# A fused attention and mixture-of-experts stage: the factors' hand-out as two fp32r products, the second layer ahead of the third, single buffers where there were pairs

## What is computed

```
edge_attn = leaky_relu(attn_src[:, src] + attn_dst[:, dst], 0.2)
p         = exp(edge_attn - max)                       # per edge and head
out       = segment_sum(p * h[src], dst) / segment_sum(p, dst)   ; x = x + out + ...
h1 = relu(bn(x @ W1[e])) ; h2 = relu(bn(h1 @ W2[e])) ; y = h2 @ Wo[e] + bo[e]
x  = x + sum_e softmax(mean @ Wr)[e] * y_e             # e = 0..7
```

## Time and profile before

| | |
|---|---|
| median of 3 runs | 6956.88 us (6955.64 to 6963.28) |
| profiled execution, its own time | 6955.62 us |
| its span | 6953.9 us |
| fused stage, about | from 520 to 3920 us of the span |

### The profile page before, as it was taken

The page is one execution under the profiler, slowest core; times in us unless marked ns, Lnnn a source line. Parts: engine busy times, 40 slices in busy tenths (PEclk is TensorE's granted clock), DMA queues, the critical chain, the costliest instruction groups (busy, mean ns, idle before and its releaser), DMA issues. The chain is left out here.

```text
span 6953.9 us, 120698 instructions
## 1 busy us (share of the span) xinstructions
PE 5410.4 (78%) x32110; PEld 4819.8 (69%) x32111; DVE 4435.2 (64%) x11425; ACT 1822.9 (26%) x4253; POOL 4050.3 (58%) x4038
## 2 busy tenths in 40 slices
PE   3427999999999999999999666767676676665887
PEld 2326888888888888888888555555555555554887
DVE  4436888788878787877888444444444454444666
ACT  1301333333333333333333300000000000002554
POOL 0147666666666666666666177777777777773111
PEclk9757999999999999999999877777777777777999
DMA  4545555555455555555555144444444444443221
GB/s 122 159 127 145 139 139 134 141 132 140 131 141 135 137 137 138 136 139 138 134 140 139 38 125 128 126 128 126 128 123 123 122 118 116 118 119 108 75 76 46
DMA packets 655172, 863.42 MB, mean 124 GB/s; under 512 B 283845, under 2 KB 463511, under 8 KB 654122
## 3 DMA queue, kind: packets, MB, share of 16 engines
q0 software_dynamic: 183296, 501.40, 26.8%
q1 hardware_dynamic: 402060, 294.79, 15.3%
q10 hardware_dynamic: 69406, 61.97, 2.7%
HBM read 714.85 MB, written 155.09 MB: 125 GB/s over the span
## 5 line engine op out<-in xcount | busy, mean ns | idle before, releaser
L1228 POOL DMA_INDIRECT m_ring<-tab_a,m_src x1764 | 1965.9, 1114 | 1219.6 <-DMA m_dstb<-dst_p 692.8
L1819 POOL DMA_INDIRECT eb_rows<-tab_b,eb_src x1568 | 1491.8, 951 | 483.6 <-issue 475.9
L1990 PE MATMUL eb_acc<-eb_rows,eb_S 128*128 128x257 f32 x3528 | 1314.0, 534 | 492.8 <-DMA eb_rows<-tab_b,eb_src 477.6
L1990 PEld LDWEIGHTS eb_acc<-eb_rows,eb_S 128*128 128x128 f32 x3528 | 935.2, 280 | 727.5 <-issue 545.3
L1508 PE MATMUL m_acc<-m_V,m_S 128*128 128x264 f32 x3528 | 867.9, 392 | 0.0
L1508 PEld LDWEIGHTS m_acc<-m_V,m_S 128*128 128x128 f32 x3528 | 653.3, 193 | 93.9
L1622 ACT ACTIVATE mh_full<-m_ps,bn_b,bn_s 128x256 f32<-128x256 f32 x784 | 400.0, 561 | 1189.5 <-DVE mh_low L509 942.5
L509 DVE TENSOR_TENSOR mh_low<-mh_full,mh_high 128x512 fp32r<-128x512 f32 x784 | 541.2, 690 | 154.1 <-ACT mh_full L1633 140.6
L1633 ACT ACTIVATE mh_high<-m_ps,bn_b,bn_s 128x256 fp32r<-128x256 f32 x784 | 441.3, 563 | 702.5 <-PE m_ps L521 702.5
L1304 DVE TENSOR_TENSOR m_V<-m_ring,m_V 128x1280 f32<-128x1280 f32 (+1 forms) x392 | 532.5, 1359 | 57.9 <-DVE m_V L1301 0.5
L521 PE MATMUL m_psY<-mWo_low,mh_high 128*128 128x256 f32 x1568 | 350.5, 305 | 255.7 <-issue 240.5
(11 more groups left out here) (348 smaller groups left out, 10716.5 us busy)
## 6 DMA issues: line engine op xcount, KB each, us to landing
m_dstb<-dst_p SPq DMA_DIRECT2D x196, 320.0 KB
m_dstb<-dst_p SPq DMA_DIRECT2D x196, 256.0 KB
buf<-fill SPq DMA_DIRECT2D x49, 771.0 KB
m_ring<-tab_a,m_src POOLq DMA_INDIRECT x1764
eb_rows<-tab_b,eb_src POOLq DMA_INDIRECT x1568, 2.8
xw_stage<-in_L_ffn_w_dram ACTq DMA_DIRECT2D x16, 1024.0 KB, 8.6
over<-b_blank SPq DMA_DIRECT2D x9, 1452.0 KB, 15.1
mOV<-over SPq DMA_DIRECT2D x49, 264.0 KB, 4.4
```

Source lines behind the costliest of these rows:

```text
L1228: gp.indirect_dma_start(out=ring[:, j, :], out_offset=None, in_=scratch["tab_a"], in_offset=bass.IndirectOffsetOnAxis(ap=src[:, j:j + 1], ...
L1819: gp.indirect_dma_start(out=rows_[par][:, to, 0:D], out_offset=None, in_=scratch["tab_b"], in_offset=bass.IndirectOffsetOnAxis(ap=index[:, ...
L1990: return nc.tensor.matmul(ps_acc[par][:, 0:NR], S[par][:, j, :], rows_[par][:, j, :], start=start, stop=False)
```

## The change

1. The factors are split into `q_parts` (high and low, fp32r) in `bounds`: a ScalarE copy and a VectorE subtraction. `ST` becomes fp32r, and `hand_out` does two fp32r products for each edge tile (low, then high) in place of one fp32 matmul.
2. TensorE's order in a step becomes `layer1(e+1)`, `hand_out(e+1)`, [`turn`, `router`], `layer2(e)`, `layer3(e-1)`, `sum_up(e-1)`. In step 0 `layer3` of the previous group goes behind `sum_up`. VectorE's and ScalarE's orders stay.
3. `U` has one buffer (its writer waits for `x1_ok` one group later), `XL` lies in `OV`'s memory (the next `OV` is loaded at step 6 once `turn` has read `XL`, not at step 4), and `fill` is gone: the rows that clear `buf` come from a table in DRAM, `empty`, which `bounds` writes with three more DMAs.

```diff
@@ bounds @@
+            with nc.allow_non_contiguous_dma(reason="one value a row"):
+                for lo, hi, of in ((0, D, blank[:, 0:D]), (D, 2 * D + 1, blank[:, 0:D + 1]), (2 * D + 1, XW, far[:, :])):
+                    sp.dma_start(scratch["empty"][:, lo:hi], of).then_inc(blanked, 16)
...
+            v.wait_ge(q_high, 1)
+            step(k["q_parts"].lower(nc, k["q"][:, 0:NT, :]))
...
+            s.wait_ge(q_ok, 2)
+            nc.scalar.copy(k["q_parts"].high[:, :, :], k["q"][:, 0:NT, :]).then_inc(q_high, 1)
@@ attend_mix, SyncE @@
-                at_least(sp, over_ok, q.n)
+                at_least(sp, T_ok, q.n)
...
-                    if e == 4 and after and not (isinstance(q.n, int) and q.n + 2 >= Q):
+                    if e == 6 and after and not (isinstance(q.n, int) and q.n + 2 >= Q):
                         load(q.next().next())
                     if e == 6:
...
-                                     fill[:, :].rearrange("p (x f) -> p x f", x=1).to_broadcast([P, FILL, XW])).then_inc(filled, 16)
+                                     scratch["empty"].rearrange("p (x f) -> p x f", x=1).to_broadcast([P, FILL, XW])).then_inc(filled, 16)
@@ attend_mix, TensorE @@
                 for j in range(s.size):
-                    last_i = nc.tensor.matmul(psE[s.side][:, j * 16:j * 16 + 2 * H], ST[s.side][:, j, :],
-                                              k["q"][:, bass.ds(s.n, 1), :].rearrange("p x c -> p (x c)"), start=True, stop=True)
+                    for i, part in enumerate(reversed(k["q_parts"].at(bass.ds(s.n, 1)))):
+                        last_i = nc.tensor.matmul(psE[s.side][:, j * 16:j * 16 + 2 * H], ST[s.side][:, j, :],
+                                                  part.rearrange("p x c -> p (x c)"), start=i == 0, stop=i == 1)
...
                     hand_out(Slot(q, e + 1))
-                    if e:
-                        layer3(q, e - 1)
-                    elif before:
-                        layer3(q.prev(), NX - 1)
...
                     if e == 0:
                         sum_up(Slot(q, -1))
+                        if before:
+                            layer3(q.prev(), NX - 1)
                         output_bias(q)
                         layer1(q, 1)
                     layer2(q, e)
                     if e:
+                        layer3(q, e - 1)
                         sum_up(Slot(q, e - 1))
@@ attend_mix, ScalarE @@
-                at_least(s, x1_ok, q.n - 1)
+                at_least(s, x1_ok, q.n)
                 hold(s, passed)
-                nc.scalar.copy(U[q.par][:, j, :], ps_acc[at.par][:, 0:NA]).then_inc(U_ok, 1)
+                nc.scalar.copy(U[:, j, :], ps_acc[at.par][:, 0:NA]).then_inc(U_ok, 1)
```

More of the change, by code:

```diff
@@ L124, in build @@
             k["bn_b"] = [sbuf(first, f"bn_b{i}", [P, NX * KB]) for i in range(2)]
-            k["q"] = sbuf(first, "q", [P, NT + 1, 2 * H])
+            k["q_parts"] = Split(sbuf, first, "q", [P, NT, 2 * H])
             k["corr"] = sbuf(first, "corr", [P, NT, H])
             with ExitStack() as early:
+                k["q"] = sbuf(early, "q_full", [P, NT + 1, 2 * H])
                 k["sd"] = sbuf(early, "sd", [P, NT, 2 * H])
@@ L556, in bounds @@
     blank = sbuf(ctx, "b_blank", [P, NA])
+    far = sbuf(ctx, "b_far", [P, 1])
     node_i = sbuf(ctx, "b_node_i", [P, NT], I32)
@@ L596, in bounds @@
         "cand_ok", "col_ps", "col_ok", "pos_ps", "hot_ok", "list_ps", "list_ok"))
+    q_high = s_("q_high")
     staged, ST_ok, z_ps, z_dv, z_done, dv, passed = map(s_, ("staged", "ST_ok", "z_ps", "z_dv", "z_done", "dv", "passed"))
@@ L660, in _ @@
             rest()
-            sp.wait_ge(blank_ok, 1)
+            sp.wait_ge(blank_ok, 2)
+            with nc.allow_non_contiguous_dma(reason="one value a row"):
+                for lo, hi, of in ((0, D, blank[:, 0:D]), (D, 2 * D + 1, blank[:, 0:D + 1]), (2 * D + 1, XW, far[:, :])):
+                    sp.dma_start(scratch["empty"][:, lo:hi], of).then_inc(blanked, 16)
             for g in range(9):
@@ L664, in _ @@
                              blank[:, :].rearrange("p (x f) -> p x f", x=1).to_broadcast([P, 11, NA])).then_inc(blanked, 16)
-            sp.wait_ge(blanked, 16 * 9)
+            sp.wait_ge(blanked, 16 * 12)
             sp.wait_ge(pp_out, 16)
@@ L730, in _ @@
             nc.vector.memset(blank[:, :], 0.0).then_inc(blank_ok, 1)
+            nc.vector.memset(far[:, :], float(FAR)).then_inc(blank_ok, 1)
             step(nc.vector.memset(zrun[:, :, :], -HUGE))
@@ L1080, in attend_mix @@
     mhalf = sbuf(ctx, "mhalf4", [P, GM])
-    fill = sbuf(ctx, "fill", [P, XW])
     ring = sbuf(ctx, "m_ring", [P, WT, TA])
@@ L1086, in attend_mix @@
     dstb = [sbuf(ctx, f"m_dstb{i}", [P, QUARTERS[i] * P], I32) for i in pair]
-    ST = [sbuf(ctx, f"m_ST{i}", [P, QUARTERS[i], P]) for i in pair]
+    ST = [sbuf(ctx, f"m_ST{i}", [P, QUARTERS[i], P], F32R) for i in pair]
     V = [sbuf(ctx, f"m_V{i}", [P, QUARTERS[i], NA]) for i in pair]
@@ L1092, in attend_mix @@
     node_col = [sbuf(ctx, f"m_col{i}", [P, 1]) for i in pair]
-    U = [sbuf(ctx, f"mU{i}", [P, GM, NA]) for i in pair]
-    OV = sbuf(ctx, "mOV", [P, GM, NA])
+    U = sbuf(ctx, "mU", [P, GM, NA])
     R = [sbuf(ctx, f"mR{i}", [P, GM, D]) for i in pair]
     den = [sbuf(ctx, f"mden{i}", [P, GM, H]) for i in pair]
-    XL = sbuf(ctx, "mXL", [P, GM, D])
+    OV = sbuf(ctx, "mOV", [P, GM, NA])
+    XL = OV[:, :, 0:D]
     XL2 = sbuf(ctx, "mXM", [P, GM, D])
@@ L1133, in attend_mix @@
     x2_out = [s_(f"x2_out{i}") for i in pair]
-    passed, filled, fill_ok = map(s_, ("passed", "filled", "fill_ok"))
+    passed, filled = map(s_, ("passed", "filled"))
     h1_high, XT_low, h1_low, h2_low = map(s_, ("h1_high", "XT_low", "h1_low", "h2_low"))
@@ L1206, in _ @@
                 first_turn(sp, k, x2_out[i], 2)
-            sp.wait_ge(fill_ok, 2)
             groups(sp, body)
@@ L1217, in _ @@
             gp.iota(col_i[:, :], [[P, 1]], base=0, channel_multiplier=1).then_inc(const, 1)
-            gp.memset(fill[:, 0:XW - 1], 0.0).then_inc(fill_ok, 1)
-            gp.memset(fill[:, XW - 1:XW], float(FAR)).then_inc(fill_ok, 1)
             gp.wait_ge(const, 2)
@@ L1348, in attended @@
                 hold(v, passed)
-                nc.vector.tensor_tensor(U[p][:, :, :], U[p][:, :, :], OV[:, :, :], ADD).then_inc(over_ok, 1)
+                nc.vector.tensor_tensor(U[:, :, :], U[:, :, :], OV[:, :, :], ADD).then_inc(over_ok, 1)
                 v.wait_ge(over_ok, q.n + 1)
                 hold(v, passed)
-                nc.vector.tensor_tensor(den[p][:, :, :], U[p][:, :, D:NA], corr[:, bass.ds(q.n * GM, GM), :], ADD)\
+                nc.vector.tensor_tensor(den[p][:, :, :], U[:, :, D:NA], corr[:, bass.ds(q.n * GM, GM), :], ADD)\
                     .then_inc(den_ok, 1)
@@ L1358, in attended @@
                 nc.vector.tensor_tensor(
-                    U[p][:, :, 0:D].rearrange("p t (h o) -> p t h o", h=H),
-                    U[p][:, :, 0:D].rearrange("p t (h o) -> p t h o", h=H),
+                    U[:, :, 0:D].rearrange("p t (h o) -> p t h o", h=H),
+                    U[:, :, 0:D].rearrange("p t (h o) -> p t h o", h=H),
                     den[p][:, :, :].rearrange("p t (h x) -> p t h x", x=1).to_broadcast([P, GM, H, HD]), MUL)\
@@ L1366, in front_start @@
                 v.wait_ge(att_ok, q.n + 1)
-                nc.vector.tensor_tensor(R[p][:, :, :], R[p][:, :, :], U[p][:, :, 0:D], ADD).then_inc(x1_ok, 1)
+                nc.vector.tensor_tensor(R[p][:, :, :], R[p][:, :, :], U[:, :, 0:D], ADD).then_inc(x1_ok, 1)
                 v.wait_ge(x1_ok, q.n + 1)
@@ L2430 @@
         "L1_ffn_w1", "L1_ffn_b1", "L1_ffn_w2", "L1_ffn_b2"]
-_SCRATCH = {"tab_a": (NP, TA), "tab_s": (NP, H), "resid_a": (NP, D), "over": (NP + P, NA), "x2": (NP, D),
+_SCRATCH = {"tab_a": (NP, TA), "tab_s": (NP, H), "resid_a": (NP, D), "over": (NP + P, NA), "empty": (P, XW), "x2": (NP, D),
             "tab_b": (NP, D), "buf": (NT // GM * FILL * P, XW),
```

## The result

The changed kernel takes 7662.94 us in the median (7649.96 to 7680.13, 4 runs), the kernel before 6956.26 us beside it: a ratio of 1.1016, 95% interval 1.0992 to 1.104. That is 706 us slower. The direction and the place were as forecast; the loss was twice the forecast's 358 us (7314), and the time lies outside its range of 7200 to 7395.

A forecast was written before the change was run, and what follows sets the result against it. The prediction took a closed loop of waits between TensorE and VectorE in the fused stage as the bound: 338 (47 groups) + 16 (last two groups) + 4 (bounds) = +358 on 6955.6, 7314 us, range 7200 to 7395.

The forecast's parts named there:

- the loop: Fused stage: sum of edges, build, low_h2, low_h1, second layer, third layer, sum; the old loop with low_h1's 1.06 us added.
- late extras: VectorE's extra work delaying later steps: attended 0.95 us into step 3, front_start 0.4 into step 4, low_XT with softmax_start 0.1.
- the two layers 2.92: TensorE's second and third layers, on the loop in each step, taken as 2.92 us together.
- rival 3: TensorE's clock falls more often: one more dip a group, 47 x 1.4 = +66 us, 7380 us; chance 13%.
- the stretch of 3866 to 3910: Last groups, without edges: TensorE 72% busy at clock 1.00, stalls of 1.49 us included; taken as speaking against more clock dips.
- The loop's price: Fused stage: +7.2 us a group, +338 us over 47 groups; with +16 for the last two groups and +4 in bounds, +358.
- busy share of 0.84: Sign in the profile after: TensorE's busy share between 1500 and 2500 us falls to about 0.84.
- the wait before the add: Sign in the profile after: VectorE newly waits some 0.7 us before the add for the third layer.
- The hand-out: TensorE's edge-tile products, two instructions a tile as before, at about 0.12 us each: no change.
- ST in fp32r: VectorE's build of ST: takes as long as before, 1.40 us for 640 columns; no change.
- bounds: The stage that splits the factors and writes the blank rows: +4 us (0 to 8).
- The buffers: Single U, XL in OV's memory and the clearing from DRAM: no wait, zero us.

The follow-up runs named there:

- experiment 1: Two runs: the kernel before with only TensorE's new order, 7657.36 us (1.1004); the changed kernel with the old order, 6981.48 us (1.0033).
- experiment 2: The changed kernel with useless products in TensorE's stall: all of them, 7380.21 us (1.0609); a third of them, on slow chips, 8436.62 us (1.064) in the third run.
- filler: The changed kernel with 74 useless fp32r products a group in TensorE's stall before the second layer, 7380.21 us (1.0609).
- old_order: The changed kernel with TensorE's order of before; fp32r hand-out, split factors, single buffers and clearing from DRAM stay: 6981.48 us (1.0033).
- low_h1_first: The changed kernel with VectorE's low_h1(e) moved ahead of build(e+2) in steps 1 to 7: 6937.82 us (0.9973), and 6938.42 us the second time.
- before_again: The kernel before, unchanged, run once for a profile on a slow chip: 7895.35 us.

## Why the prediction was wrong

- **What bounds the kernel, and the loop: right.** The stall moved to the second layer, the add waits for the third layer, and the order alone carries the loss (experiment 1). Where the clock was at 1.00, from the sum's end to the second layer took 4.37, 4.74 and 4.99 us in steps 2 to 4 (experiment 2), against 4.40, 3.57 + 0.95 and 4.40 + 0.4 in the forecast: within 0.2 us, the late extras included.
- **The step that failed: "the two layers 2.92", taken at the full clock in every step.** The layers lie on the loop, so what a dip takes from them lengthens the step. The sum gave new dips no time; the forecast had them as rival 3, priced at one more dip of 1.4 us a group, +66 us, with a chance of 13%. The granted clock fell from 0.98 to 0.90 in a group of 82.0 us: that is some 16 us at half speed a group where it was 2.7, and the filler puts its price at 283 us, four times that of the rival. It belonged in the sum.
- **The row that misled** was the stretch of 3866 to 3910, 72% busy at 1.00. It has no hand-outs, so that none of its stalls, one of them 2.91 us long, is behind one. The trace of before had the nearer rows: of its 50 stalls over 1.0 us behind a hand-out, 27 had a dip, the one of the earlier trace rows among them. The forecast itself put such stalls into most steps. An estimate from these counts: five a group (234 after the change, in 47 groups), a dip behind every second one, and 1.7 us lost by each (half of the 3.4 us from 2067.04 to 2070.45, of which the forecast saw 2.8), come to some 215 us. The Trainium skill ("TensorE: Matmul & The Clock Gate", Part 1: The HAM clock gate) says that the throttled clock is the default and activity releases it. The forecast noted that by this rule rival 3 was the likelier one, and the filler's run agrees with it: 74 more products a group, and 0.98 in place of 0.90.
- **The loop's price** was 424 us against 358. In the filler run steps 3 and 4 were 0.2 us each longer than laid out, some 20 us. The end of the two-group loop was left out of the sum: the idle time before the first layer's first products, nearly all of it there, is 48.6 us in the filler run and 12.8 in the kernel before, 36 us more. In the changed kernel without the filler it is 20.9. I did not try that by itself.
- **Two of the signs.** TensorE's busy share of 0.84 came as forecast, but by luck: at half the clock the same products are busy for longer, and the count of instructions fell to 0.83 of before's. At the full clock 14.1 us more a group would have left a share near 0.76. And the wait before the add was put at 0.7 us a step; it is 2.0 (788.5 over 392).
- **The hand-out: right.** Its instructions lie 0.11 us apart, in fp32r as before. **ST in fp32r: right**, 1.36 us. **bounds: right**, the stage's first load went from 520.59 to 524.47 us, +3.9 for +4.
- **The buffers: nearly.** `old_order` costs 26 us, 4 of them before the first output bias (648.2 against 644.4); the other 22 were forecast as zero. They lie at the start of a turn of the two-group loop: TensorE's idle time there, before the first layer's first products, is 40.9 us where it was 12.8, in 21 stalls of 0.81 to 4.23 us. Why is open: no wait for `U`, `OV` or the clearing of `buf` shows.

## What to carry to other kernels

When an order is changed between engines, write down the closed loop of waits before and after, operation by operation: what the change takes off the loop counts less than what the unchanged order of the other engine puts on it. Where TensorE's work lies on that loop, price the clock as well: count in the old trace how often a stall of the same kind, behind the same work, already has a stretch at half the clock, and multiply by the new stalls. Neither a mean busy share nor a stretch with other work in it stands in for that. Here the waits alone gave 5% and the measured loss was 10%. And the cheap repair was on the other engine: what is waited for first goes first, and work with a whole step of slack goes behind it.

## What the runs showed that was not expected

- Useless products made a kernel faster: 74 a group, on an engine that already limits the stage, took 283 us off, with TensorE's clock back at 0.98. On a slow chip a third of them gave about a third of the gain.
- VectorE's first instruction of a new turn of the two-group loop came 3.5 to 4.3 us behind the last of the turn before (4.25 us in the changed kernel, 3.54 in `low_h1_first`, 3.97 in the kernel before, one turn read in each), with nothing that the profile names in between.
- On the slow chips the same program took 7895 to 8081 us. In the one profile of it there (`before_again`) the mean-aggregating stage moved 91 GB/s where it was 118, and the fused stage had a clock of 0.96 with single stalls of over 3 us. A sixth of the time went with the chip that a run got; why is open.
